# State sums of the third sequence on TensorE, and three PSUM banks instead of four for two more FFNs

## What is computed

```python
# Mamba: 256 inner channels, 16 states each
dA = exp(A * delta_t);  new = dA * state + delta_t * B_t * h_t
y = einsum('bin,bn->bi', new, C_t) + D * h_t       # the sum over 16 states
out = (y * silu(gate)) @ out_w + out_b             # "gating", then m_out
# mixture: softmax router, top 2 of 8 experts, 128 -> 352 -> 128, all 8 computed
out = sum_e w_e * ((up_e(x) * silu(gate_e(x))) @ w_down[e])
```

## Time and profile before

| | before |
|---|---|
| median of 3 runs | 655.52 us (655.02 to 658.4) |
| the profiled execution | 658.64 us |
| its span | 656.8 us |
| TensorE busy | 601.8 us, 92% |
| VectorE busy | 519.5 us, 79% |
| ScalarE busy | 384.1 us, 58% |
| GpSimd busy | 375.2 us, 57% |
| mean granted TensorE clock | 0.961 |

### The profile page before, as it was taken

How to read it: one execution, slowest core, us unless ns; L and a number is a source line. 1 busy time by engine, 2 the same in 40 slices (tenths; PEclk the granted TensorE clock), 3 DMA queues, 4 the chain that set the end, 5 groups by cost and what they waited for, 6 DMA issues and landing times.

```text
span 656.8 us, 13047 instructions
## 1 busy us (share of the span) xinstructions
PE 601.8 (92%) x4536; PEld 557.0 (85%) x4536; DVE 519.5 (79%) x1164; ACT 384.1 (58%) x794; POOL 375.2 (57%) x321
## 2 busy tenths in 40 slices
PE   6479799879989999999999999899999999999998
PEld 5224588469889999999999999899989999999998
DVE  5599578977798889988998899879988896445454
ACT  5886545636658675777567755667476641515230
POOL 1097263559686597869686977597674765000000
PEclk9579699979989999999999999899999999999999
DMA  8733023103021211222030303030304000000000
GB/s 288 247 119 130 1 76 132 65 4 137 3 97 45 85 68 30 113 73 80 9 133 19 133 3 140 13 137 3 141 1 147 3 13 8 15 1 13 1 21 9
DMA packets 18163, 45.31 MB, mean 69 GB/s; under 512 B 2799, under 2 KB 13488, under 8 KB 13746
## 3 DMA queue, kind: packets, MB, share of 16 engines
q1 hardware_dynamic: 18098, 44.49, 19.3%
HBM read 40.02 MB, written 1.31 MB: 63 GB/s over the span
## 4 chain that ended last, share of the span: by engine, by line
PE 79%; DVE 9%; issue 4%; ACT 3%; POOL 3%; DMA 1%; SPq 1%; DVEq 0%; ACTq 0%; POOLq 0%
PE ps L1234 23%; PE ps L1062 15%; PE ps L1063 15%; PE ps L1064 15%; DVE st L925 3%; PE ps L1184 2%; PE ps L1283 2%; POOL st L479 2%; DVE ps L911 2%; DMA inner_ring<-gate_w 1%; PE ps L1120 1%; PE ps L1129 1%; PE ps L1296 1%; DVE X L1026 1%; PE ps L1274 1%
## 5 line engine op out<-in xcount | busy, mean ns | idle before, releaser
L479 POOL TENSOR_TENSOR st<-st,rows_ring 128x512 f32<-128x512 f32 x128 | 165.4, 1296 | 100.5 <-DVE st L925 100.5
L1234 PE MATMUL ps<-down,inner_ring 128*128 128x128 f32 (+1 forms) x1408 | 171.9, 275 | 0.0
L1234 PEld LDWEIGHTS ps<-down,inner_ring 128*128 128x128 f32 (+1 forms) x1408 | 165.8, 191 | 2.2 <-issue 1.4
L713 ACT ACTIVATE sg<-ps 128x512 f32<-128x512 f32 x176 | 104.6, 595 | 106.5 <-PE ps L1064 103.6
L1012 DVE TENSOR_TENSOR inner_ring<-sg,ps 128x512 f32<-128x512 f32 x176 | 118.8, 679 | 51.3 <-PE ps L1064 24.2
L925 DVE TENSOR_TENSOR_SCAN st<-dA,ps 128x512 f32<-128x512 f32 x128 | 155.2, 1214 | 5.1 <-ACT dA L668 2.6
L492 POOL TENSOR_TENSOR yacc<-yacc,st 128x512 f32<-128x512 f32 x96 | 123.1, 1282 | 5.7
L1062 PE MATMUL ps<-xhi,gate_hi 128*128 128x256 f32 x352 | 103.9, 295 | 17.6 <-DVE xlo L962 17.6
L668 ACT ACTIVATE dA<-delta,A 128x255 f32<-128x255 f32 x256 | 105.6, 494 | 1.8 <-POOL delta L471 1.7
L1062 PE MATMUL ps<-xhi,up_hi 128*128 128x256 f32 x352 | 105.3, 299 | 1.4 <-DVE inner_ring L1012 1.4
L1064 PE MATMUL ps<-xhi,gate_lo 128*128 128x256 f32 x352 | 101.2, 287 | 0.0
(11 more groups left out here) (150 smaller groups left out, 888.3 us busy)
## 6 DMA issues: line engine op xcount, KB each, us to landing
rows_ring<-bc SPq DMA_DIRECT2D x32, 1024.0 KB, 4.9
moved_rows<-inner_ring SPq DMA_DIRECT2D x96, 32.0 KB, 1.8
inner_ring<-gate_w SPq DMA_DIRECT2D x1, 1408.0 KB, 8.9
inner_ring<-up_w SPq DMA_DIRECT2D x1, 1408.0 KB, 11.2
down<-down_w SPq DMA_DIRECT2D x2, 512.0 KB, 8.9
out<-X SPq DMA_DIRECT2D x8, 128.0 KB, 1.8
X<-x SPq DMA_DIRECT2D x1, 896.0 KB, 6.0
down<-down_w SPq DMA_DIRECT2D x1, 384.0 KB, 8.3
```

What stands on the lines that cost most here:

```text
L479: nc.gpsimd.tensor_tensor(st[:, i % NST], st[:, i % NST], row, ALU.mult).then_inc(s["m_p"], 1)
L713: nc.scalar.activation(sg[:, k % 2], two(bank_of(q, 2 * j)), ACT.Silu).then_inc(s["f_sg"], 1)
L1234: ins = nc.tensor.matmul(bank_of(q, 2 * NP + e)[:, c * H:(c + 1) * H], act_in, down[0:rows, e, n, :], start=n == 0, stop=n == NB - 1)
```

## The change

Two constants:

```diff
-NSUM = 2
+NSUM = 3
 NR0 = 3
-NARROW = 1
+NARROW = 3
```

## The result

The change made the kernel slower: 670.94 us in the median of 4 runs (670.1 to 672.02), beside 656.96 us for the kernel before (655.02 to 661.17, 4 runs: the three of the table above, with a median of 655.52, and one more of 661.17). The ratio is 1.020, with a 95% interval from 1.016 to 1.024. A second set of runs, beside the experiments, gave 1.020 again (1.016 to 1.023). The profiled execution took 670.1 us around a span of 668.1 us.

A forecast was written before the change was run, and what follows sets the result against it. TensorE's list of work was taken to bound the kernel from about 141 us on. 16.0 us on the path + 0.4 for banks - 3.4 for the clock = 13.0, so 655.5 + 13.0 = 668.5 us, +2.0%; 8-in-10 range 664 to 675.

The forecast's parts named there:

- TensorE's list is the bound, GpSimd's relief is worth 0: From about 141 us to the end TensorE's work sets the time; 21.8 us leaving GpSimd count 0.
- Sums 1 to 7 at 0.86, 6.0 us: After FFN 1's first gate product and through FFN 1, where TensorE is full: 7 x 0.86 = 6.0 us.
- sums 0, 8 and 9 in holes for nothing: Ahead of FFN 1, late in FFN 1 and ahead of FFN 2: 0 us; at most 1.5 (opening, sum 0) and 2.3.
- Sums 10 to 15 with zeros at 1.44, 8.6 us: Between gate and up products of FFN 2, where TensorE is full: 6 x 1.44 = 8.6 us.
- The six products, 1.34 us: Products after m_out of sequence 2, amid down products: 12 records of 128 columns, 1.34 us on the path.
- Products ready, scans not held: GpSimd's products come before the sums' places, and scans don't wait for sums: 0 us, for scans a few tenths possible.
- Gating on VectorE, 0: One 0.69 us operation after inner product 10 of FFN 2, waiting for sum 15: 0 us, at most 0.7.
- Three banks, 0.4 us: In FFN 1 and 2 gate product j needs inner product j-2's bank: 0.4 us for both, range 0 to 3.
- a sign of being wrong: In the profile after: gate products waiting for inner products, new waits for GpSimd's product, or shorter periods after 215 us.
- The clock gives back 3.4 us: Filled holes ahead of FFN 1 and 2 return 1.7 us at each; bounds 5.1 back to 1.7 more lost.
- cost half of that, 3.4 and 1.7 us of work: Half-clock falls of 6.8 us at FFN 1 and 3.4 us at FFN 2 were priced at half their length.
- the signs that were named: In the profile after: sum counts, full TensorE, clock 1.00 around 186 to 194 us, shorter holes, later FFN 2 and followers.

The follow-up runs named there:

- the doubled list: Three banks; TensorE gets the change's whole list with operands that wait for nothing, GpSimd still makes the real sums; ratio 1.0178 against the kernel before, +11.7 us.
- the relief alone: Kernel before, four banks, with the third sequence's sums left out on every engine; ratio 0.999 (0.996 to 1.002).
- the two later fills: Kernel before with unread products after m_out of sequence 1 and ahead of each FFN from FFN 2, without or with ten more ahead of FFN 0; ratios 0.994 and 0.9945.
- the filled kernel: Kernel before with unread products in two holes: eight more after m_out of sequence 1, six ahead of FFN 2's first gate product; ratio 0.9964, 2.4 us faster.

## Why the prediction was right, and which terms were off

The forecast was 668.5 us and +13.0; measured were 670.9 and a ratio that makes +13.1 us of 656.96, or 14.0 by the medians. The two FFNs alone show +14.2. That forecast and result lie within about 1 us is in part luck: the errors below are up to 1.6 us each, and some cancel. Point by point:

- **TensorE's list is the bound, GpSimd's relief is worth 0.** Shown, by the doubled list (46.31 and 42.28 us against 46.36 and 42.29) and by the relief alone (0.0 us).
- **Sums 1 to 7 at 0.86, 6.0 us; sums 0, 8 and 9 in holes for nothing.** Shown. With the clock at 1.00 on both sides the stretch from FFN 1 to FFN 2 is 40.33 us without sums and 46.36 with them: 6.03 us. (With 40.70, of the two later fills, it is 5.7. The change has a wait of 0.63 us for a bank in it where the filled kernels have 0.17 and 0.53, so the exact 7 x 0.86 = 6.0 is a little lucky.) FFN 1's first gate product still waited 1.01 us for xlo, and from m_out on it took 6.48 us as against 6.47, so the opening and sum 0 cost nothing. The holes at FFN 2 shrank from 1.51 and 1.84 to 0.65 and 0.21 us, by 0.86 and 1.63, which is just what was put in.
- **Sums 10 to 15 with zeros at 1.44, 8.6 us.** The mechanism was right, the size too small. A sum behind zeros takes 1.05 us, so it is 6 x 1.63 = 9.8 us. The chain of before had this already in the first sequence's sums, where the 0.58 at 51.31 comes from too (the prediction calls it the second's): the pieces behind its zeros took 1.06 and 1.07 us where I had taken 0.86 from a stream without zeros.

```profile
51.89 1.06 PE ps L1184 x2
...
54.39 1.07 PE ps L1184 x2
```

- **The six products, 1.34 us.** They belong to the 5.2 us that went with the zeros in FFN 2. Not measured by themselves; from the first down product to FFN 3's first gate product it took 15.53 us in the change (from 210.99) and 14.43 in the filled kernel (from 196.45), 1.1 more.
- **Products ready, scans not held.** Shown: TensorE has no wait for GpSimd in the two FFNs, and no scan there waits for a sum.
- **Gating on VectorE, 0.** It waited 0.89 us for sum 15, and m_out followed the down products without idle time. Timeline of VectorE after:

```profile
211.19 0.69 DVE L934 TENSOR_TENSOR yacc<-ps,gact 128x512 f32<-128x512 f32 x1 [0.89 <-PE ps L1184]
```

- **Three banks, 0.4 us.** Two waits, 0.8 us, in the change. The prediction named such waits as a sign of being wrong; two came, 0.8 us where 0.4 had been taken. Alone +1.0 us, within the noise, and 3.4 us in the one profile, most of it without a wait that the profile shows. Against four banks with the clock up (the filled kernel had waits of 0.17 and 0.78 us for inner products) they cost nothing that can be told.
- **The clock gives back 3.4 us.** It did rise to 1.00 in both FFNs, further than I took. But the return, measured with four banks and without sums, was 1.5 to 1.8 us at FFN 1 and nothing at FFN 2, where 1.7 was taken at each. That FFN 1 fits is luck: the fall of 6.8 us had been priced at 3.4, half of it was taken back, and in fact all came back and was worth half the price. The step that failed is "cost half of that, 3.4 and 1.7 us of work": it holds only where TensorE has nothing else to wait for. In FFN 2's first pairs VectorE was only just ahead of TensorE at half clock: before the change there is no wait for an inner product, with the clock up one of 0.78 us. In FFN 1 such waits came in too (0.17 and 0.53 us), and the fall had begun ahead of the first gate product, in a hole (0.50 from 139.40, the product at 140.49); together they don't make up all that is missing of the 3.4. What the return was worth at FFN 2 with the sums between the products, no run shows.

So 16.0 + 0.4 - 3.4 stands against 6.0 + 9.8 + 1.3, with nothing for banks, less 1.8 for the clock: 15.3. The stretches show 14.2. The 1.1 us between them lies in FFN 2: 42.29 less 32.39 us of the filled kernel are 9.9, where 9.8 + 1.3 = 11.1 had been put in. In the filled kernel TensorE waits for an inner product for 0.78 us, in the change for 0.15, which makes 0.6 of it; the sums fill time that TensorE spent waiting for VectorE. The rest, 0.5 us, is not measured by itself.

Of the two misses that I can name, zeros (+1.1) and clock (+1.6), both made the forecast too low. The bounds of the clock's term (5.1 back to 1.7 lost) held what it was; the sum behind zeros had been given no bounds at all, and should have had some.

Of the signs that were named, 48 sums on TensorE and 80 on GpSimd, the clock at 1.00 and the shorter holes ahead of FFN 2 came true. FFN 2's first gate product came only 1.6 us later than before (3 to 7 were named) and FFN 3's 11.6 (12 to 14), since the clock had been up in FFN 0; counted from FFN 1's first they are 4.2 and 14.2 us.

## What to carry to other kernels

When one engine's in-order list is full, work moved onto it costs its length in the chain, however much another engine is relieved; read that length for the exact neighbours it will have, since here the same sum took 0.86 us in a plain stream and 1.05 us behind zero products. Work laid in a hole that another chain ends is free as long as it fits, at the clock that the engine has just there, and its place in the list tells beforehand which piece falls in one. And a clock that comes back gives time only as far as the next engine keeps up: look at how far the engine that empties the banks was behind before you count half of the slow time as gained.

## What the runs showed of the hardware that was not expected

- Products that nobody reads, laid in holes of 1.0 to 3.0 us ahead of each FFN from the second on, made the kernel 0.6% faster (0.992 to 0.996). They kept the granted clock at 1.00 where it had been 0.50 for 3.4 to 6.8 us at a time. The Trainium skill (TensorE: Matmul & The Clock Gate, "Why this matters for your kernels") warns of long idle gaps between bursts. Here no long one was needed: ahead of the fall at 422.7 us TensorE was idle once, for 1.16 us, and busy for the other 2.24 of 3.40 us. The like hole of 1.16 us ahead of FFN 3 (214.94) had no fall behind it, so the length of the hole alone doesn't tell.
- At a granted clock of 0.50 the filling products are twice as long: 20 records took 4.64 us, 0.23 each, against 0.11 in the earlier trace rows. A fill that is right for the full clock overruns its hole if the clock is already down.
- The clock falls in different places in executions of one kernel. From FFN 0 to FFN 1, where the lists are alike up to m_out of sequence 1, it was 0.94 before and 1.00 after. That is worth 2.3 us, and is why the spans of the two profiles differ by 11.3 us where the two FFNs cost 14.2.
